# Two graph attentions and two routed feed-forward layers: the last heads and the experts in another order, and products of zeros on TensorE before the first expert

## The reference, cut to what matters

```python
h = gat_conv(x, src, dst, W1, ..., heads=8, 128)       # h = x @ W; e = leaky_relu(a_src[src] + a_dst[dst])
h = jax.nn.relu(h)                                      # softmax of e over the edges of each dst
out = gat_conv(h, src, dst, W2, ..., heads=8, 64)       # out = sum of h[src] * alpha, + bias
x = x + jax.nn.log_softmax(out, axis=1)
...
logits = layernorm(x) @ Wr + br                         # 8 experts, each token takes one
idx = argmax(logits); gate = softmax over that one
x = x + gate * (relu(xf @ W1[idx] + b1[idx]) @ W2[idx] + b2[idx])
```

## Time and profile before

| | |
|---|---|
| median of 3 runs | 1260.65 us (1257.49 to 1263.9) |
| the profiled execution's own time | 1262.32 us |
| its span in the trace | 1260.6 us |
| mean granted clock of PE | 0.899 of 2.4 GHz |
| PE, weight load, DVE, ACT, POOL busy | 84%, 60%, 61%, 42%, 50% of the span |
| first attention, pairs | about 689 to 881 us |
| final attention, pairs | about 913 to 1163 us |
| last layer behind it | 1163 us to the end |

### The profile page before, as it was taken

How to read it: one execution, slowest core, us unless ns; L and a number is a source line. 1 busy time by engine, 2 the same in 40 slices (tenths; PEclk the granted TensorE clock), 3 DMA queues, 4 the chain that set the end, 5 groups by cost and what they waited for, 6 DMA issues and landing times. The chain is left out here.

```text
span 1260.6 us, 17829 instructions
## 1 busy us (share of the span) xinstructions
PE 1059.0 (84%) x5581; PEld 752.3 (60%) x5581; DVE 770.9 (61%) x1724; ACT 523.9 (42%) x744; POOL 624.6 (50%) x503
## 2 busy tenths in 40 slices
PE   3999899878799999995797888888888888546696
PEld 1454677767577777773454788787654444222574
DVE  6898487537233333332976799974577777725754
ACT  2243553321111111111233688887366776525323
POOL 1000549105476555544203788996587786623233
PEclk9999899755799999997798799999799899968698
DMA  3000003056489999963201112210111111621541
GB/s 113 1 0 1 1 1 134 1 185 217 145 292 301 300 304 306 300 207 122 94 1 36 32 37 67 69 35 17 45 57 45 34 51 34 185 100 45 166 142 50
DMA packets 107987, 134.57 MB, mean 107 GB/s; under 512 B 30240, under 2 KB 76040, under 8 KB 107792
## 3 DMA queue, kind: packets, MB, share of 16 engines
q1 hardware_dynamic: 92720, 112.68, 27.7%
q0 software_dynamic: 15200, 21.04, 5.1%
HBM read 135.03 MB, written 27.45 MB: 129 GB/s over the span
## 5 line engine op out<-in xcount | busy, mean ns | idle before, releaser
L2306 POOL TENSOR_TENSOR am<-CT,qb 128x1024 f32<-128x1024 f32 x128 | 301.7, 2370 | 100.8 <-ACT PT L2335 79.6
L2328 ACT ACTIVATE PS<-adb,ab 128x1024 f32<-128x1024 f32 x128 | 143.1, 1118 | 126.1 <-DVE am L2433 125.0
L2539 PE MATMUL PS<-PT,h 128*65 128x512 f32 x256 | 134.9, 667 | 57.6 <-ACT PT L2335 38.7
L2433 DVE TENSOR_TENSOR am<-PS,am 128x1024 f32<-128x1024 f32 x128 | 156.5, 1222 | 39.9 <-ACT PS L2328 27.8
L2427 DVE CUSTOM_DVE_ANT_0 masked<-PS,mask 128x1024 f32<-128x1024 f32 x128 | 156.2, 1220 | 35.7 <-issue 34.0
L2526 PE MATMUL PS<-h,PT 128*128 128x129 f32 x1024 | 131.2, 287 | 22.6 <-DVE o L2458 11.4
L1232 DVE COPY yo<-PS 128x512 f32<-128x512 f32 x64 | 44.3, 692 | 168.5 <-PE PS L1170 163.1
L2335 ACT ACTIVATE PT<-am,as 128x1024 f32<-128x1024 f32 x128 | 145.1, 1134 | 0.3 <-DVE am L2433 0.3
L2526 PEld LDWEIGHTS PS<-h,PT 128*128 128x128 f32 x1024 | 124.6, 200 | 30.4 <-issue 19.4
L1197 ACT ACTIVATE hT<-PS,b1T 128x128 f32<-128x128 f32 x128 | 40.0, 363 | 215.2 <-PE PS L1162 199.9
L1162 PE MATMUL PS<-xgT,w1r 128*128 128x128 f32 x1024 | 126.1, 277 | 0.0
(11 more groups left out here) (421 smaller groups left out, 1726.3 us busy)
## 6 DMA issues: line engine op xcount, KB each, us to landing
w2r<-in_L_ffn_W SPq DMA_DIRECT2D x64, 512.0 KB
w1r<-in_L_ffn_W SPq DMA_DIRECT2D x64, 512.0 KB
adb<-a_scratch SPq DMA_DIRECT2D x16, 512.0 KB, 3.9
qb<-q_scratch SPq DMA_DIRECT2D x14, 512.0 KB, 4.9
wc<-in_L_gnn_W SPq DMA_DIRECT2D x4, 1024.0 KB, 8.4
w1x<-in_L_ffn_W SPq DMA_DIRECT2D x2, 2048.0 KB, 10.3
w2x<-in_L_ffn_W SPq DMA_DIRECT2D x2, 2048.0 KB, 9.1
w1x<-in_L_ffn_W SPq DMA_DIRECT2D x7, 512.0 KB, 4.0
```

The lines of the kernel that those rows point to most:

```text
L2306: pool.tensor_tensor(am[:, k % RING, :], CT[:, s, :], qb[:, hd % 2, :], ALU.add).then_inc(s_sum, 1)
L2328: act.activation(RELU, adb[:, hd % 2, :], ACT.Relu, bias=ab[:, s, hd:hd + 1]).then_inc(s_relu, 1)
L2433: dve.tensor_tensor(am[:, k % RING, :], RELU, am[:, k % RING, :], ALU.add).then_inc(s_all, 1)
L2539: mm = pe.matmul(PS[0:CH + 1, half, :], h[:, s, hd, :], PT[:, (NT * hd + s) % PR, half * 512:(half + 1) * 512], start=(s == 0), stop=(s == ...
```

## The change

In the last heads TURN, SUM and the copies have new places, and the copies have a table of their own (MOVE). In the final attention oT is copied in halves, with a semaphore s_half for the first. q comes two pairs earlier in both attentions. In the first attention the unit H0 - 1 is copied before the pairs. PE gets products of zeros at four places of its end (41 in all). On DVE the last layer's small steps are reordered: integer steps before the first norm, norms one block further ahead, `places` behind block 0, `owners` behind block 2; the gates of blocks are done earlier (`gated_at`), and of the last block everything but its product is computed before (s_rest), so that one instruction follows PE.

```diff
-            TURN = {(6, 2): (0, 0), (6, 4): (0, 1), (6, 5): (1, 0), (6, 6): (1, 1), (6, 7): (2, 0), (7, 0): (2, 1)}
-            SUM = {(6, 4): (0, 0), (6, 5): (0, 1), (6, 6): (1, 0), (6, 7): (1, 1), (7, 0): (2, 0), (7, 1): (2, 1)}
+            TURN = {(6, 2): (0, 0), (6, 4): (0, 1), (6, 6): (1, 0), (7, 0): (1, 1), (7, 2): (2, 0), (7, 4): (2, 1)}
+            SUM = {(6, 3): (0, 0), (6, 5): (0, 1), (6, 7): (1, 0), (7, 1): (1, 1), (7, 3): (2, 0), (7, 5): (2, 1)}
+            MOVE = {(6, 4): (0, 0), (6, 6): (0, 1), (7, 0): (1, 0), (7, 2): (1, 1), (7, 4): (2, 0), (7, 6): (2, 1)}
...
+            def gated_at(self, e):
+                return {0: (), 1: (), 2: (), 3: (0,), 4: (1, 2), 5: (3, 4)}.get(e, (e - 1,))
...
                 def store(e):
-                    pool.wait_ge(self.s_fin, e + 1)
+                    if e < NB1 - 1:
+                        pool.wait_ge(self.s_fin, e + 1)
+                    else:
+                        pool.wait_ge(self.s_last, 1)
...
                     a.then_inc(self.s_hhm, 1)
-                    if e >= 3:
-                        finished(e - 3)
-                for e in range(NB1 - 3, NB1):
-                    finished(e)
+                    if e == NB1 - 1:
+                        act.wait_ge(self.s_rest, 1)
+                        g = self.xg8[:, e % self.G8, :]
+                        act.activation(g, g, ACT.Identity, bias=self.sc[:, 2, e:e + 1]).then_inc(self.s_restm, 1)
+                    for i in self.gated_at(e):
+                        finished(i)
...
+            def zeros(self, pe, n):
+                for _ in range(n):
+                    pe.matmul(PS[:, 0, :], onesb[:], zerob[:], start=True, stop=True)
             def pe_end(self, pe):
+                self.zeros(pe, 7)
                 pe.wait_ge(self.s_xp, 8)
...
                 pe.matmul(PS[:, 6, 0:(NT + 1) * NX1], onesb[:], zerob[:, 0:(NT + 1) * NX1], start=True, stop=False)
+                self.zeros(pe, 9)
                 pe.wait_ge(self.s_pick, 1)
...
                 mm.then_inc(self.s_rank, 1)
+                self.zeros(pe, 3)
                 pe.wait_ge(self.s_rhs, 1)
...
                 pe.wait_ge(self.s_w1[1], 16)
+                self.zeros(pe, 22)
                 turn(0)
...
-                ev = {(6, 3): (0, 0), (6, 4): (0, 1), (6, 5): (1, 0), (6, 6): (1, 1), (6, 7): (2, 0), (7, 0): (2, 1)}
-                if (hd, s) in ev:
-                    self.x_moved(dve, *ev[hd, s])
+                if (hd, s) in self.MOVE:
+                    self.x_moved(dve, *self.MOVE[hd, s])
...
-                normed(0)
-                normed(1)
-                turned(0)
                 link(dve.tensor_copy(self.rki[:], self.rk[:]))
...
+                normed(0)
+                normed(1)
+                turned(0)
                 normed(2)
...
                 link(i)
+                turned(1)
+                normed(3)
+                def places():
...
+                def owners():
...
-                    if e and e + 2 < NB1:
-                        normed(e + 2)
+                    if e and e + 3 < NB1:
+                        normed(e + 3)
                     if e:
                         moved(e - 1, ofs[e - 1])
+                    if e == 0:
+                        places()
+                    if e == 2:
+                        owners()
...
-                    if e >= 3:
-                        gated(e - 3)
-                gated(NB1 - 3)
-                gated(NB1 - 2)
-                moved(NB1 - 1, ofs[NB1 - 1])
-                gated(NB1 - 1)
+                    for i in self.gated_at(e):
+                        gated(i)
+                    if e == NB1 - 2:
+                        n = NB1 - 1
+                        g = self.xg8[:, n % self.G8, :]
+                        dve.wait_ge(self.s_xn, NB1)
+                        dve.scalar_tensor_tensor(g, self.b2b[...], self.sc[:, 3, n:n + 1], g, ALU.mult, ALU.add
+                                                 ).then_inc(self.s_rest, 1)
+                n = NB1 - 1
+                dve.wait_ge(self.s_y, NB1)
+                dve.wait_ge(self.s_restm, 1)
+                dve.wait_ge(self.s_st[n % 4], 16 * (n // 4))
+                dve.scalar_tensor_tensor(self.yo4[:, n % 4, :], PS[:, 4 + n % 2, :], self.sc[:, 3, n:n + 1],
+                                         self.xg8[:, n % self.G8, :], ALU.mult, ALU.add).then_inc(self.s_last, 1)
...
-            Q_AFTER = {1: 1, **{NT * (hd - 1) + 2: hd for hd in range(2, HEADS)}}
+            Q_AFTER = {1: 1, **{NT * (hd - 1): hd for hd in range(2, HEADS)}}
...
                     def moved(hd):
-                        act.wait_ge(s_O, NT * hd + NT)
                         wait(act, s_tr, hd)
-                        act.copy(oT[:], PS[0:CH + 1, 0:2, :].rearrange("p a n -> p (a n)")).then_inc(s_oT, 1)
+                        for half in range(2):
+                            act.wait_ge(s_half if half == 0 else s_O, hd + 1 if half == 0 else NT * hd + NT)
+                            act.copy(oT[:, half * 512:(half + 1) * 512], PS[0:CH + 1, half, :]).then_inc(s_oT, 1)
...
-                    for i in range(max(2, H0 - 3), H0 - 1):
+                    for i in range(max(2, H0 - 3), H0 - 1 if final else H0):
                         h_moved(i, unit_bank(i))
...
-                        if k == 0:
+                        if final and k == 0:
                             h_moved(H0 - 1, unit_bank(H0 - 1))
...
                     def columns(hd, s):
-                        if s == 0:
-                            wait(pe, s_oT, hd)
...
                         for half in range(2):
+                            if s == 0:
+                                wait(pe, s_oT, 2 * hd - 1 + half)
                             mm = pe.matmul(...)
+                            if half == 0 and s == NT - 1:
+                                mm.then_inc(s_half, 1)
                         mm.then_inc(s_O, 1)
```

More of the change, by code:

```diff
@@ L2068, in dve_end @@
                 link(i)
-                link(dve.tensor_scalar(self.col[:], self.hif[:], 0.0, -64.0, ALU.is_equal, ALU.mult))
-                link(dve.tensor_tensor(self.begt[:], self.begt[:], self.hif[:], ALU.add))
-                link(dve.scalar_tensor_tensor(self.col[:], self.begt[:], -1.0, self.col[:], ALU.add, ALU.add))
-                link(dve.tensor_tensor(self.Mc[:], self.jx[:, :, 0:1].rearrange("p j o -> p (j o)").unsqueeze(1).to_broadcast(
-                    [P, NT, MORE]), rows(self.col, MORE), ALU.is_equal))
@@ L2075, in dve_end @@
-                link(dve.tensor_scalar(self.lof[:], self.hif[:], 0.0, None, ALU.is_equal))
-                link(dve.tensor_tensor(self.Mf[:], self.M[:], rows(self.lof), ALU.mult))
-                for n, v in ((0, self.tok), (1, self.d0), (2, self.rx)):
-                    dve.tensor_tensor(self.rhs2[:, :, W + n * MORE:W + (n + 1) * MORE], self.Mc[:], rows(v, MORE), ALU.mult)
-                link(dve.tensor_tensor(self.jc[:], self.jx[:], self.cum[:].unsqueeze(1).to_broadcast([P, MORE, NX1]),
-                                       ALU.is_ge))
@@ L2094, in dve_end @@
+                def owners():
+                    link(dve.tensor_tensor(self.jc[:], self.jx[:], self.cum[:].unsqueeze(1).to_broadcast([P, MORE, NX1]),
+                                           ALU.is_ge))
+                    link(dve.tensor_reduce(self.own[:], self.jc[:], X, ALU.add))
+                    link(dve.tensor_scalar(self.own[:], self.own[:], float(NX1 - 1), None, ALU.min))
+                    dve.tensor_copy(self.owni[:], self.own[:]).then_inc(self.s_own, 1)
                 ofs = {}
@@ L2111, in dve_end @@
                         dve.wait_ge(self.s_scal, 1)
[L2112 to L2117 removed]
+                    for i in self.gated_at(e):
[4 more added lines that the diff above has]
+                        dve.wait_ge(self.s_xn, NB1)
+                        dve.scalar_tensor_tensor(g, self.b2b[:, self.expert(dve, n), :].rearrange("p o d -> p (o d)"),
+                                                 self.sc[:, 3, n:n + 1], g, ALU.mult, ALU.add).then_inc(self.s_rest, 1)
+                n = NB1 - 1
[4 more added lines that the diff above has]
+                                         self.xg8[:, n % self.G8, :], ALU.mult, ALU.add).then_inc(self.s_last, 1)
             def biased_end(self, dve):
```

41 lines of the change are left out of this document (25 added, 16 removed).

## The result

The changed kernel took 1222.43 us (median of 4, 1216.82 to 1227.64), the one before 1262.24 beside it (4 runs): a ratio of 0.969, 95% interval 0.9638 to 0.9741. A second set of five runs gave 0.9699 (0.9679 to 0.972). The forecast was 1221 (1207 to 1240). The profiled execution has a span of 1220.4 us for 1260.6 and a mean granted clock of 0.926.

What follows compares the result with a forecast made beforehand. The prediction saw a full circle of waits between DVE, ACT and PE in the last heads. Terms of 26, 2.4, 1.8, 2.5, 3.1, 1.6 and 3.5 sum to 40.9 us off 1262.3, giving 1221 us, range 1207 to 1240.

Steps and rivals of the forecast that it cites:

- The last heads: Heads 6 and 7 of the second attention: turns two pairs apart, copies two pairs behind; 26 us less, between 16 and 37.
- the free end: Last heads: the gain if POOL's additions hold none of DVE's instructions, 37 us less.
- the holding: Last heads: POOL's additions hold DVE instructions with two SBUF inputs; eight at 1.33 us, 11 us, between nothing and 21.
- Rival A: Last heads: DVE isn't held by POOL in the new rhythm; 11 us less, 1210 us; chance 0.20.
- B: Last heads: PE doesn't keep its clock, 16 us less than 83, and zeros come 4 late; 1236 us; chance 0.12.
- The halves: Head starts and the last head's end: oT copied in halves lets PE start 0.4 us earlier; 2.4 us, 0 to 4.
- q and the unit's copy: First attention: earlier q gains 1.8 us (0 to 2.3), the unit's copy before the loop 2.5 (0 to 3.7).
- Zeros and the order up to the third expert: From the last heads into the experts: zeros lift PE's clock, 3.1 us (-5 to 4.4); DVE's order gains 1.6 (0 to 3.4).
- all fit at full clock: Between heads and experts: the 41 products of zeros fit PE's four idle places; at half clock 22 are 4 us late.
- Owners comes later, but its seven loads have 20 us. From there PE is full: Experts: naming the owners later delays nothing, and PE is full at 3.94 us an expert; no gain there.
- The end: Behind PE's end: one 0.74 us instruction remains, the last store starts at +1.8; 3.5 us less (2 to 4.3).
- the circle: Last heads: DVE's copy waits for PE's transposes, the next scores stand behind it, no pairs overlap; DVE stood 34.0 us.

Runs made afterwards that it cites:

- experiments 1 and 2: old_order (old order put back in the kernel after), 1254.16 us, and only_order (new order alone in the kernel before), 1234.72 us.
- after_again: The kernel after run once more, nothing changed: 1224.8 us, ratio 0.9699 to the kernel before.
- experiments 2 and 10: only_order (new order alone in the kernel before), 1234.72 us, and whole_oT (oT copied whole in the kernel after), 1224.81 us.
- only_order: The kernel before with only the new places of turns, sums and moves in heads 6 and 7: 1234.72 us, ratio 0.9744.
- whole_oT: The kernel after with oT of the second attention copied whole again instead of by halves: 1224.81 us, one run.
- more_mid: The kernel after with 12 products of zeros for 9 before the selection and 6 for 3 before the table: 1225.76 us, ratio 0.9697.
- psum_bias: The kernel after with 384 bias columns copied once into PSUM and read there by the maxima of heads 6 and 7: 1214.5 us, ratio 0.9601.
- old_order: The kernel after with turns, sums and moves of heads 6 and 7 put back to their old places: 1254.16 us, ratio 0.9897.
- one_input: The kernel after with three quarters of the maxima reading z alone, the bias addition left out there: 1210.74 us, ratio 0.955.
- no_zeros: The kernel after without one product of zeros: 1224.39 us, ratio 0.9675.
- old_q: The kernel after with q of every head after the first computed two pairs later, in its old place: 1223.8 us, one run.

## Why the prediction was right, and where it was off

**The last heads**: 26 us forecast; the order alone is 23.6 to 28.8, by the profiles that are compared (experiments 1 and 2). The mechanism holds at each step. From 81.6 us the free end, 37 less, would have left 44.6, and the full 26 less leaves 55.6; it took 54.6 (56.8 in after_again). The difference is the holding, 11 us forecast as eight pieces at 1.33. In the trace the maxima's 14.0 us are 9.0 more than with the bias in PSUM (five pieces held by 1.5 to 2.1 us each), and of the three x_res from (6,4) on one was held, by 1.0 (1.67 us at 1089.72): 10.0 in all, six pieces, fewer and longer. The x_res ahead of (6,4) were held before too, and stand in the 44.6. Taking the first part away gave 8 to 9, and the stretch was 46.1, near the free end, x_res still being held. Rival A (no holding) is out, B too: the clock in the stretch was 0.91.

**The halves**: forecast 2.4; measured 0.5 at the end of the last head, and inside the attention nothing that the runs can tell from their spread (experiments 2 and 10). The step in doubt is "with halves PE starts 0.4 earlier", taken as a gain for five heads. PE does start 0.4 earlier, but the next pair begins sooner only if PE is the bound there, and the prediction gave no row for that. only_order, without halves, passed heads 1 to 5 as fast as any kernel with them; whole_oT did not. The term stays open between 0 and 2 us.

**q and the unit's copy**: q 2.3 for 1.8, at the upper bound of 2.3. The copy 5.0 for 2.5, above the bound of 3.7. The bound was DVE's idle time alone. The prediction names the half clock there, but gave no price to its length: with the late start it ends some 5 us later, 0.82 for 0.95 over 20 us. In the second attention q did what was forecast: it waits in GpSimd for the last maximum (4.47 us at 1066.02), and with q in its old place the attention took 244.5 us, within the spread.

**Zeros and the order up to the third expert**: 3.1 + 1.6 forecast, 2.2 measured from the last column product to TensorE's end (87.5 to 85.3 us), 0.5 of which are the halves' at the last head. Two steps failed. First, "all fit at full clock": the clock fell at the table in spite of them, the table took 3.14 us, and the last 22 ran 1.5 us past the first rows. Where it held, 22 was the right number (4.9 us in more_mid and psum_bias). With it fell the sign "clock near 1.00 from the last head to the first expert". Second, "Owners comes later, but its seven loads have 20 us. From there PE is full": the loads now go out in a burst, the ninth block's gather lands in it, and DVE waits 2.7 us. It cost TensorE less than that: 4.76 us between two W1 products for 3.94, 0.8 lost. The first product by W2 lost another 1.0, waiting for ScalarE (0.6 before): its softmax, forecast to end some 5 us before its first relu is needed, ended 0.4 us before. W1 of the third expert starts 16.1 us behind the table's end, for 17.1 before and 15.5 forecast. What is gained ahead of the experts can be lost in them, as in more_mid, but need not be: psum_bias takes 19.8 us to the first expert and 62.7 from there, 2.8 less in sum than the kernel after.

**The end**: 3.5 forecast, 2.5 measured, the same in all kernels with the change (7.9 us for 10.4). The last store starts 2.75 us behind PE, not 1.8: the store before it started 1.46 behind PE instead of 0.5.

**The sum**: 40.9 forecast, 40.2 measured in the profiled pair, with errors of both signs: the first attention gave 3.4 more than forecast (7.7 for 4.3), the second 0.8 more (28.8 for 26 and the halves' 2.0); from the last head to TensorE's end came 2.9 less (2.2 for 5.1, the halves' 0.4 with it), the end 1.0 less, and 1.0 was lost ahead of the attentions. That the numbers meet within 1.4 us is partly luck; the main term and its two parts, the circle and the holding, are shown.

## What to carry to other kernels

When a chain of waits runs in a circle through three engines, setting request and answer two steps apart can take out the whole wait (34 us here, 27 of them off the time), and it makes the next limit visible at once: look at the durations of the engine that fills up, not only at its waits. If VectorE's operations with two operands in SBUF swell from 0.4 to 2.5 us beside GpSimd, putting one operand into a free piece of PSUM is a small edit (8 to 9 us here). And a wait of an engine that isn't the bound is no gain: DVE's 2.0 us for the gather cost TensorE 0.2 in psum_bias. Subtract only where the next operation of the bounding engine moves. Last, compare a stretch over several profiles before a cause is given to a few us: the place of the clock's fall, read from two, came out otherwise in nine.

## What I had not expected of the hardware

- The same VectorE operation, 256 wide, took 1088 ns in the mean with both operands in SBUF and 417 with one of them in PSUM, beside the same GpSimd additions; 738 and 285 at 128 wide.
- With 19 products of zeros in the gaps between heads and experts the granted clock fell to 0.50 in eight of nine profiles, but at different places and for 3 to 7 us; without zeros it stayed at 0.50 for 20 to 24 us in all four.
- ScalarE began its first relu of the experts 3.3 us behind its last softmax operation in the kernel after (1154.47), though TensorE had its product at 1151.5, and 0.9 us behind it in after_again. The long pause, 2.9 to 3.3 us, is there in seven of the 14 profiles (before, after, old_order, one_input, no_zeros, more_mid, old_q), and in more_mid TensorE waits 2.29 us for it. Its cause is open.
